# New operation orders on every engine, the three gelus of a step side by side, and TensorE's instruction alignment at place 92 of 256

## The chip, the cores and the metric

The kernel runs on 1 core of one Trainium2 chip. Its engines are TensorE (PE), VectorE (DVE), ScalarE (ACT), GpSimd (POOL) and SyncE (SP), each with an instruction stream of its own; they wait for each other through semaphores. The metric is the device time of one execution in microseconds; lower is better.

## The reference

The input is x of 8 sequences x 256 tokens x 128 channels. It is normalised to xn. The output is x + attention(xn) + local(xn). The first is one plain attention of width 128. The second is a stack of six layers, each of an attention over windows of 32 tokens and a gated feed-forward layer:

```python
for i in range(DEPTH):   # 6
    x = attn_layer(shift_tokens(x), Wqkv[i], q_scale[i], k_scale[i], Wo[i]) + x
    x = ffn_layer(shift_tokens(x), ln_g[i], ln_b[i], W1[i], b1[i], W2[i], b2[i]) + x
```

`attn_layer` projects to q, k and v (16 heads of 64), scales q and k to unit length, rotates them, takes a softmax over the window and the one before it, applies v, and projects out. `ffn_layer` normalises, projects to 2 x 341 channels (a and gate), multiplies a by gelu(gate) and projects down to 128. `shift_tokens` moves half of the channels by one token. All of it is fp32.

## The kernel before, in words

The plain attention is done first (about the first 50 us) and isn't touched. Then 48 **steps** follow, one for each layer and sequence: step n is layer n // 8 of sequence n % 8. A step's tokens are two tiles of 128. Every engine has a function `iteration(n)`, called for n = 0 to 52, in which the operations are written out by hand in a fixed order, each with the step that it belongs to: `hidden(n - 5, 1)` works on the step five back. So five or six steps are in flight, and an engine never takes an operation out of turn: one that waits holds up all behind it on its engine. `live(n)` leaves out steps that don't exist, at the beginning (the fill) and at the end (the drain).

TensorE's operations of a step, with the engine that takes each result:
- `take_in`: 2 transposes of the shifted tokens; `take_x` (ScalarE, L614) rounds them to x_hi, `rest` (VectorE, L883) writes the remainder x_lo, and signals s_xl.
- `project` 0 to 7 (q and k) and `project_v` 0 to 3: 3 matmuls of 128x512 each, in fp32r (hi x hi, hi x lo, lo x hi). q and k are squared on ScalarE (`square`), summed on VectorE (`squares`), rotated on VectorE (`rotate`, L894), added and scaled on GpSimd (`add`, `scale`); v is copied by ScalarE (`copy_v`) and moved by 32 tokens by SyncE's DMAs (`copy_v0`, `copy_v1`).
- `turn_qk` 0 to 7: 4 transposes each; ScalarE copies (`take_qk`, L646).
- `scores` 0, 1: 8 matmuls with the mask and 128 of 64x64 each; VectorE takes maxima (`maxima`, `less_max`), ScalarE the exponent (`exps`), VectorE sums and reciprocals, GpSimd divides.
- `turn_p` 0 to 3: 4 transposes; ScalarE copies (`take_p`).
- `values` 0 to 3: 32 matmuls of 64 columns; ScalarE copies (`take_o`, L691).
- `project_out` 0, 1: 16 matmuls; VectorE adds into x (`middle`). SyncE loads the shifted tokens (`load_xs`), VectorE takes statistics (`stats`, `moments`), GpSimd normalises.
- `turn_normal`: 2 transposes; `affine` on ScalarE.
- `hidden` 0 to 2: 4 matmuls; ScalarE's `gelu` (L706), VectorE's `gated` (L966), then `down` (12 matmuls) and `finish`.

A matmul of fp32 operands that is no transpose is issued as two, and each of those counted here has a weight load of its own; so a step has 544 matmuls and 544 weight loads, 36 of each in the projections, 272 in the two `scores`.

There are 8 PSUM banks. The constants `QK_BANK`, `T_BANK`, `H_BANK` and so on say which bank an operation writes, and `freed(...)` ahead of a TensorE operation waits until the last reader of that bank is done:

```python
def freed(*uses):
    for signal, n, *place in uses:
        if live(n):
            pe.wait_ge(signal, upto(place[0], n, place[1]) if place else done(n))
            return
```

ScalarE holds one table of functions at a time. Gelu is in one table; exponent, logarithm and the rest are in the other. `exp_and_log()` (L610) loads the second by hand; the load of the gelu table is put ahead of a gelu that finds another table (it has that gelu's line, L706). Squares and copies work with either.

TensorE's order before, from `take_in` (steps: 0 is n, -1 is n - 1 and so on): take_in 0; turn_qk 0 and 1 of -1; project 7 of -1; down -5; turn_qk 2 of -1; turn_p 1 of -2; project 0; turn_normal -4; values 0, 1 of -2; turn_qk 3 of -1; project_v 1 of -1; project 1, 2; project_v 0 and scores 0 of -1; hidden 0 of -4; project 3; turn_p 2, 3 and project_out 0 of -2; turn_qk 6 of -1; project 4; hidden 1 of -4; turn_qk 7, 4 of -1; and in the next iteration, up to its take_in: values 3, 2 of -3; turn_qk 5 of -2; project_v 3, 2 of -2; project 5 of -1; scores 1 of -2; hidden 2 of -5; project 6 of -1; turn_p 0 of -2; project_out 1 of -3.

## Time and profile before

| what | value |
|---|---|
| time, median of 3 runs | 1537.56 us (1534.16 to 1537.81) |
| the profiled execution: time, span | 1533.61 us, 1531.8 us |
| busy share of the span | PE 97%, PEld 83%, DVE 87%, ACT 90%, POOL 81% |
| matmuls, and as many weight loads | 26320 |

The span goes from the first to the last profiled instruction of one execution. PE is TensorE's matmuls, PEld its weight loads, which overlap them. Times in the timeline are us from the span's start; a row merges equal instructions (x4) and shows in brackets how long the engine was idle before it and what released it; "issue" means that nothing in the profile did.

### The profile page before, as it was taken

Reading aid. Unit: us, or ns where it says so; the run is one execution under the profiler, and the core shown is the slowest. Engines: PE = TensorE matmul, PEld = TensorE weight load, DVE = VectorE, ACT = ScalarE, POOL = GpSimd, SP = SyncE. Lnnn points to the kernel's source line nnn. Section 1 sums busy time; section 2 is a strip of 40 time slices with the busy share of each in tenths; the row PEclk is TensorE's granted clock in tenths of the full one; section 3 lists DMA queues with packets and bytes.
Section 4 is the critical chain, followed back from the end, with each engine's and each line's share of the span. In section 5 each row is a group of like instructions: output and inputs, shape, how many; then the busy total and the mean of one; then the engine's idle time right before and its main releaser. Section 6 shows DMA issues by size and latency. Waiting matters only on the chain.

```text
span 1531.8 us, 66396 instructions
## 1 busy us (share of the span) xinstructions
PE 1480.4 (97%) x26320; PEld 1278.3 (83%) x26320; DVE 1327.0 (87%) x2365; ACT 1381.5 (90%) x2647; POOL 1242.3 (81%) x1213
## 2 busy tenths in 40 slices
PE   6689999999999999999999999999999999999996
PEld 5568888888888888888888888888888888888885
DVE  6789998898989888988988898988889898889872
ACT  4578999999999999999999999999999999999996
POOL 5588888878888888888888888888888888887861
PEclk9999999999999999999999999999999999999998
DMA  6111221212121211222121213111121211111120
GB/s 181 36 44 44 54 54 51 53 35 57 48 61 52 67 39 42 61 58 62 45 59 34 54 48 80 51 49 49 35 53 42 63 35 48 37 47 44 40 53 19
DMA packets 96161, 79.89 MB, mean 52 GB/s; under 512 B 66282, under 2 KB 79598, under 8 KB 95854
## 3 DMA queue, kind: packets, MB, share of 16 engines
q1 hardware_dynamic: 94990, 75.34, 18.8%
q8 instruction: 217, 3.56, 1.0%
q14 instruction: 90, 0.74, 0.2%
q10 hardware_dynamic: 864, 0.26, 0.1%
HBM read 17.91 MB, written 1.05 MB: 12 GB/s over the span
## 4 chain that ended last, share of the span: by engine, by line
PE 91%; issue 4%; ACT 2%; DVE 2%; POOL 1%; DMA 0%; ACTq 0%; DVEq 0%; POOLq 0%
PE bank L1075 73%; PE bank L1190 11%; PE bank L1228 5%; PE bank L1160 1%; PE bank L1262 1%; DVE n L904 0%; DMA rot<-in_b_v 0%; ACT L611 0%; POOL rot L459 0%; ACT ot L691 0%; DVE es L935 0%; DVE parts L894 0%; DVE am L828 0%; ACTq L545 0%; POOL w_lo L446 0%
## 5 line engine op out<-in xcount | busy, mean ns | idle before, releaser
L459 POOL TENSOR_TENSOR rot<-parts 128x512 f32<-128x512 f32 x384 | 493.5, 1286 | 204.9 <-DVE parts L894 204.9
L894 DVE TENSOR_TENSOR parts<-bank,rtab 128x1024 f32<-128x1024 f32 x384 | 465.5, 1213 | 0.4 <-POOL rot L459 0.3
L470 POOL TENSOR_TENSOR rot<-rot,rnorm 128x512 f32<-128x512 f32 x384 | 391.0, 1046 | 0.4 <-DVE rnorm L920 0.4
L1075 PE MATMUL bank<-w_hi,x_hi 128*128 128x512 f32 x576 | 266.6, 463 | 7.4 <-DVE parts L894 4.9
L904 DVE TENSOR_REDUCE n<-sq 128x8 f32<-128x512 f32 x384 | 255.6, 667 | 18.6 <-ACT sq L622 18.6
L622 ACT ACTIVATE sq<-bank 128x512 f32<-128x512 f32 x384 | 231.3, 602 | 38.4 <-PE bank L1075 31.0
L684 ACT ACTIVATE pz<-bank 64x512 f32<-64x512 f32 x384 | 225.8, 588 | 3.8 <-PE bank L1228 0.4
L1075 PE MATMUL bank<-w_hi,x_lo 128*128 128x512 f32 x576 | 228.5, 397 | 0.0
L1075 PE MATMUL bank<-w_lo,x_hi 128*128 128x512 f32 x576 | 228.0, 396 | 0.0
L476 POOL TENSOR_TENSOR es<-es,r 128x512 f32<-128x512 f32 x192 | 200.5, 1045 | 28.3 <-DVE r L946 28.2
L1190 PE MATMUL bank<-ident,rot 128*128 128x128 f32 x1536 | 220.4, 276 | 2.3 <-POOL rot L470 1.8
L1075 PE MATMUL bank<-w_o,ot 128*128 128x128 f32 x1536 | 187.5, 275 | 0.0
L1190 PEld LDWEIGHTS bank<-ident,rot 128*128 128x128 f32 x1536 | 173.8, 141 | 15.8 <-issue 1.8
L1075 PEld LDWEIGHTS bank<-w_o,ot 128*128 128x128 f32 x1536 | 179.2, 192 | 0.5 <-issue 0.4
L935 DVE TENSOR_TENSOR es<-bank,m 128x512 f32<-128x512 f32 x192 | 127.5, 685 | 45.5 <-PE bank L1228 45.5
L646 ACT ACTIVATE kt<-bank 128x512 f32<-128x512 f32 x192 | 113.7, 592 | 53.2 <-PE bank L1190 52.4
L1075 PE MATMUL bank<-xg,w 128*128 128x256 f32 (+1 forms) x576 | 157.3, 396 | 4.3 <-DVE ht L970 2.2
L1075 PEld LDWEIGHTS bank<-kt,qt 64*32 64x32 f32 x12288 | 139.2, 105 | 10.7 <-issue 6.3
L1075 PE MATMUL bank<-kt,qt 64*32 64x64 f32 x12288 | 141.3, 225 | 5.5 <-issue 5.5
L929 DVE TENSOR_REDUCE m<-bank 128x8 f32<-128x512 f32 x192 | 126.5, 679 | 7.9 <-PE bank L1075 7.3
L1075 PEld LDWEIGHTS bank<-w_hi,x_lo 128*128 128x128 f32 x576 | 108.8, 189 | 26.6
L1075 PEld LDWEIGHTS bank<-w_hi,x_hi 128*128 128x128 f32 x576 | 109.1, 189 | 24.9 <-DVE parts L894 5.6
(86 smaller groups left out, 2799.9 us busy)
## 6 DMA issues: line engine op xcount, KB each, us to landing
vb<-v SPq DMA_DIRECT2D x96, 384.0 KB, 4.0
w_new<-in_Wqkv SPq DMA_DIRECT2D x36, 256.0 KB, 4.0
vb<-v SPq DMA_DIRECT2D x48, 128.0 KB, 2.6
w_o<-in_Wo SPq DMA_DIRECT2D x12, 256.0 KB
xin<-x_tok SPq DMA_DIRECT2D x48, 64.0 KB, 2.1
xs<-x_tok SPq DMA_DIRECT2D x48, 64.0 KB, 2.0
xin<-x_tok SPq DMA_DIRECT2D x48, 56.0 KB, 3.0
xs<-x_tok SPq DMA_DIRECT2D x48, 56.0 KB, 3.1
```

The costliest lines, as they stand in the source:

```text
L459: g.tensor_tensor(rot[:, i * CH:(i + 1) * CH].rearrange(halves, z=2, c=HD), parts[:, b:b + CH].rearrange(halves, z=2, c=HD), parts[:, b + ...
L470: g.tensor_tensor(c, c, over(r, CHH, DH), ALU.mult).then_inc(s_sc[i], 1)
L476: g.tensor_tensor(e, e, over(r8[:, (u % 2) * PAIRS:(u % 2 + 1) * PAIRS], PAIRS, DH), ALU.mult)\
L622: a.activation(sq[:, (i % 2) * CH:(i % 2 + 1) * CH], bank[QK_BANK[i]][:, :], ACT.Square)\
L646: a.activation(dst, bank[T_BANK[i]][:, :].rearrange("p (a t) -> p a t", a=4), ACT.Copy)\
L684: last = a.activation(pz4[r, u % 2, s, :], bank[P_BANK[u]][r, :], ACT.Copy)
L894: d.tensor_tensor(parts[:, b:b + 2 * CH].rearrange("p (w h c) -> p w h c", w=2, c=DH), heads(bank[QK_BANK[i]][:, :]).unsqueeze(1).to_broad ...
L904: d.tensor_reduce(n2[:, T * 2 * HEADS + m * CHH:T * 2 * HEADS + (m + 1) * CHH], heads(sq[:, b:b + CH]), op=ALU.add, axis=AX.X).then_inc(s_ ...
L929: d.tensor_reduce(eight(m8, u), heads(bank[S_BANK[u // 2][u % 2]][:, :]), op=ALU.max, axis=AX.X)\
L935: d.tensor_tensor(heads(es[:, (u % 2) * CH:(u % 2 + 1) * CH]), heads(bank[S_BANK[u // 2][u % 2]][:, :]), over(eight(m8, u), PAIRS, DH), AL ...
L1075: return t.matmul(o, l, r, start=start, stop=stop, skip_group_check=True)
L1190: last = t.transpose(bank[T_BANK[i]][:, k * P:(k + 1) * P], rot[:, i * CH + k * P:i * CH + (k + 1) * P], ident[:, :])
```

## The change

Every engine's order in `iteration` is written anew, with the banks and waits that belong to it. No arithmetic is added or taken away. ScalarE's three gelus now follow each other but for two copies, so that one load of the gelu table and one `exp_and_log` are left in a step. `align_block` is called from iteration 0 on, with 92 of 256 for 42 of 128.

TensorE's order after, from `take_in`: take_in 0; turn_p 1 of -2; project 6, 7 and turn_qk 0 of -1; project 0; down -5; values 0, 1 of -2; project 1; turn_qk 2, 1, 3 of -1; turn_normal -4; project_v 0 of -1; project 3; turn_p 2 of -2; project 2; project_v 1 and scores 0 of -1; project 4; turn_p 3 of -2; and in the next iteration, up to its take_in: project_out 0 of -3; turn_qk 4, 6, 5 of -2; values 2, 3 of -3; turn_qk 7 of -2; project 5 of -1; project_v 2 of -2; hidden 1 of -5; scores 1, turn_p 0 and project_v 3 of -2; hidden 2, 0 of -5; project_out 1 of -3.

VectorE's order after begins with the maxima of -2 and ends with squares 3 of n; `rest` stands behind gated 1, 2, 0 and squares 4. GpSimd's begins with scale 5, 7 of -2 and add 1 of -1 and ends with add 0 of n and scale 4, 6 of -1. The diff, cut to SyncE, ScalarE, and the parts of TensorE's order around the new alignment, hidden and down:

```diff
 DEEP = 5
-BLOCK, SLOT = 128, 42
+BLOCK, SLOT = 256, 92
 SPLIT_FROM = 2
 PARTS = ((0, 1), (1, 3), (3, SEQS))
-QK_BANK, T_BANK = (1, 3, 0, 5, 6, 5, 2, 3), (4, 5, 0, 6, 2, 3, 2, 7)
-V_BANK, P_BANK, O_BANK = (5, 4, 4, 1), (0, 4, 2, 7), (0, 7, 0, 4)
-S_BANK, W_BANK, H_BANK = ((6, 1), (7, 6)), (3, 3), (4, 1, 1)
-XIN_BANK, N_BANK, D_BANK = 1, 2, 1
-LAST_N2, LAST_SC = (3, 7), (3, 5)
+QK_BANK, T_BANK = (1, 3, 0, 7, 4, 2, 4, 0), (3, 4, 7, 2, 1, 6, 3, 6)
+V_BANK, P_BANK, O_BANK = (5, 1, 1, 1), (4, 5, 4, 3), (6, 5, 2, 0)
+S_BANK, W_BANK, H_BANK = ((6, 2), (6, 7)), (5, 2), (0, 3, 5)
+XIN_BANK, N_BANK, D_BANK = 3, 0, 2
+LAST_N2, LAST_SC = (2, 7), (3, 7)
...
@@ -382,15 +382,15 @@
                 if live(n):
                     load_x(n)
                 if live(n - 2):
-                    copy_v0(n - 2)
-                if live(n - 4):
-                    load_xs(n - 4)
-                if live(n - 2):
                     copy_v1(n - 2)
+                if live(n - 3):
+                    load_xs(n - 3)
+                if live(n - 1):
+                    copy_v0(n - 1)
                 if live(n - 5):
                     later_weights(n - 5)
-                if live(n - 2):
-                    later_qkv(n - 2)
+                if live(n - 1):
+                    later_qkv(n - 1)
...
             def take_x(n):
                 act.wait_ge(s_xt, done(n))
-                act.wait_ge(s_vp[2], done(n - 2))
+                act.wait_ge(s_vp[3], done(n - 2))
                 a.activation(buffer(x_hi, n, LEN), bank[XIN_BANK][:, 0:LEN], ACT.Copy).then_inc(s_xh, 1)
...
             exp_and_log()
 
             def iteration(n):
-                if live(n - 5):
-                    gelu(n - 5, 0)
-                if live(n - 1):
-                    square(n - 1, 3)
                 if live(n - 3):
-                    take_p(n - 3, 2)
                     take_p(n - 3, 3)
                 if live(n - 2):
+                    exps(n - 2, 0)
+                if live(n):
+                    next_hi(n)
+                if live(n - 2):
                     take_qk(n - 2, 6)
-                if live(n - 1):
+                    exps(n - 2, 1)
+                    take_qk(n - 2, 5)
+                    take_qk(n - 2, 4)
+                if live(n - 3):
+                    take_o(n - 3, 2)
+                if live(n - 1):
+                    guard(n - 1, 0)
                     square(n - 1, 4)
-                    guard(n - 1, 0)
+                if live(n - 2):
+                    take_qk(n - 2, 7)
+                if live(n - 1):
+                    square(n - 1, 5)
+                if live(n - 3):
+                    take_o(n - 3, 3)
+                if live(n - 1):
+                    logarithm(n - 1, 0)
+                if live(n - 2):
+                    copy_v(n - 2, 2)
+                if live(n - 1):
+                    first_root(n - 1, 0)
+                    half_square(n - 1, 0)
                 if live(n - 5):
                     gelu(n - 5, 1)
-                    exp_and_log()
-                if live(n - 1):
-                    logarithm(n - 1, 0)
-                if live(n - 2):
-                    exps(n - 2, 0)
-                if live(n - 3):
-                    take_o(n - 3, 3)
-                if live(n - 2):
-                    exps(n - 2, 1)
-                if live(n - 1):
-                    first_root(n - 1, 0)
-                    half_square(n - 1, 0)
-                if live(n - 2):
-                    take_qk(n - 2, 7)
-                    take_qk(n - 2, 5)
-                    take_qk(n - 2, 4)
+                if live(n - 2):
+                    take_p(n - 2, 0)
                     copy_v(n - 2, 3)
-                if live(n - 1):
-                    square(n - 1, 5)
-                if live(n - 2):
-                    copy_v(n - 2, 2)
-                if live(n - 3):
-                    take_o(n - 3, 2)
                 if live(n - 5):
                     gelu(n - 5, 2)
+                    gelu(n - 5, 0)
                     exp_and_log()
+                if live(n):
+                    take_x(n)
+                if live(n - 2):
+                    exps(n - 2, 2)
+                    take_p(n - 2, 1)
                 if live(n - 1):
                     square(n - 1, 6)
-                if live(n - 2):
-                    take_p(n - 2, 0)
-                if live(n):
-                    take_x(n)
-                if live(n - 1):
+                    square(n - 1, 7)
                     take_qk(n - 1, 0)
-                if live(n - 2):
-                    exps(n - 2, 2)
-                if live(n - 1):
-                    square(n - 1, 7)
+                if live(n):
+                    square(n, 0)
+                if live(n - 2):
+                    exps(n - 2, 3)
+                    take_o(n - 2, 0)
+                if live(n - 1):
+                    guard(n - 1, 1)
+                if live(n - 2):
+                    take_o(n - 2, 1)
+                if live(n - 1):
+                    logarithm(n - 1, 1)
                     take_qk(n - 1, 2)
-                if live(n - 2):
-                    take_p(n - 2, 1)
-                if live(n - 1):
                     take_qk(n - 1, 1)
-                    guard(n - 1, 1)
-                if live(n):
-                    square(n, 0)
-                if live(n - 1):
-                    logarithm(n - 1, 1)
                     first_root(n - 1, 1)
-                if live(n - 2):
-                    exps(n - 2, 3)
-                if live(n - 1):
                     half_square(n - 1, 1)
-                if live(n - 2):
-                    take_o(n - 2, 0)
-                if live(n - 1):
-                    take_qk(n - 1, 3)
-                if live(n):
-                    square(n, 1)
-                if live(n - 1):
-                    copy_v(n - 1, 1)
                 if live(n - 4):
                     affine(n - 4)
                 if live(n):
...
-            def align_block(n):
-
-                if live(n - DEEP):
-                    t.addr_align(BLOCK, offset=SLOT, max_nops=0)
+            def align_block():
+
+                t.addr_align(BLOCK, offset=SLOT, max_nops=0)
 
             def take_in(n):
                 pe.wait_ge(s_xin[n % 2], 64 * (n // 2) + 64)
...
-                if live(n - 2):
-                    freed((s_mid[0], n - 3), (s_rot[1], n - 1, 8, 1))
-                    turn_qk(n - 2, 5)
-                    freed((s_hm[1], n - 5), (s_sub[1], n - 2, 4, 1))
+                if live(n - 2):
+                    freed((s_qte[5], n - 2))
+                    turn_qk(n - 2, 7)
+                if live(n - 1):
+                    freed((s_ot[2], n - 3), (s_sub[1], n - 2, 4, 1))
+                    project(n - 1, 5)
+                if live(n - 2):
+                    freed((s_qte[4], n - 2))
+                    project_v(n - 2, 2)
+                if live(n - 5):
+                    freed((s_qte[6], n - 2),
+                          (s_pte[1], n - 3, 4, 3),
+                          (s_rot[1], n - 1, 8, 1),
+                          (s_qte[0], n - 2),
+                          (s_xl, n - 1),
+                          (s_hm[1], n - 6))
+                    hidden(n - 5, 1)
+                if live(n - 2):
+                    freed((s_qte[7], n - 2))
+                    freed((s_rot[1], n - 1, 8, 3), (s_qte[2], n - 2))
+                    scores(n - 2, 1)
+                    freed((s_rot[0], n - 1, 8, 4), (s_pte[0], n - 3, 4, 2))
+                    turn_p(n - 2, 0)
+                    freed((s_v[2], n - 2))
                     project_v(n - 2, 3)
-                    freed((s_ot[3], n - 3), (s_hm[0], n - 5), (s_v[1], n - 2))
-                    project_v(n - 2, 2)
-                if live(n - 1):
-                    freed((s_rot[1], n - 1, 8, 3))
-                    project(n - 1, 5)
-                if live(n - 2):
-                    freed((s_qte[7], n - 2))
-                    freed((s_rot[0], n - 1, 8, 4), (s_sub[0], n - 2, 4, 0))
-                    scores(n - 2, 1)
                 if live(n - 5):
-                    freed((s_v[3], n - 2), (s_hm[1], n - 5))
+                    freed((s_mid[0], n - 3),
+                          (s_v[0], n - 2),
+                          (s_ot[1], n - 3),
+                          (s_pte[1], n - 3, 4, 1),
+                          (s_hm[2], n - 6))
                     hidden(n - 5, 2)
-                if live(n - 1):
-                    freed((s_qte[4], n - 2))
+                    freed((s_ot[3], n - 3), (s_rot[0], n - 1, 8, 2), (s_xg, n - 5))
+                    hidden(n - 5, 0)
+                if live(n - 3):
+                    freed((s_rot[1], n - 1, 8, 5), (s_ot[2], n - 3))
+                    project_out(n - 3, 1)
+                if live(n):
+                    align_block()
+                    freed((s_hm[1], n - 5), (s_qte[6], n - 2), (s_pte[1], n - 3, 4, 3), (s_rot[1], n - 1, 8, 1))
+                    take_in(n)
+                if live(n - 2):
+                    freed((s_hm[2], n - 5), (s_mid[0], n - 3), (s_v[0], n - 2))
+                    turn_p(n - 2, 1)
+                if live(n - 1):
+                    freed((s_pte[0], n - 2, 4, 0), (s_rot[0], n - 1, 8, 4))
                     project(n - 1, 6)
-                if live(n - 2):
...
-                    freed((s_hm[2], n - 5),
-                          (s_v[3], n - 2),
-                          (s_hm[1], n - 5),
+                    freed((s_hm[0], n - 5), (s_ot[3], n - 3), (s_rot[0], n - 1, 8, 2))
+                    project(n - 1, 7)
+                    freed((s_xl, n), (s_hm[1], n - 5))
+                    turn_qk(n - 1, 0)
+                if live(n):
+                    freed((s_v[3], n - 2), (s_v[2], n - 2), (s_qte[4], n - 2), (s_v[1], n - 2), (s_rot[0], n - 1, 8, 0))
...
+                          (s_ot[2], n - 3),
                           (s_sub[1], n - 2, 4, 1),
-                          (s_rot[0], n - 1, 8, 0))
-                    take_in(n)
-                if live(n - 1):
-                    freed((s_v[2], n - 2))
-                    turn_qk(n - 1, 0)
-                    freed((s_rot[1], n - 1, 8, 5))
+                          (s_qte[3], n - 2),
+                          (s_xready, n - 6))
+                    down(n - 5)
+                if live(n - 2):
+                    freed((s_sub[0], n - 2, 4, 2))
+                    values(n - 2, 0)
+                    freed((s_pte[1], n - 2, 4, 1))
+                    values(n - 2, 1)
+                if live(n):
+                    freed((s_qte[0], n - 1), (s_xl, n))
+                    project(n, 1)
```

## Rows read from the trace of the kernel before

**Rows 1.** The page: busy time of the engines; the chain that ended last.
```profile
PE 1480.4 (97%) x26320; PEld 1278.3 (83%) x26320; DVE 1327.0 (87%) x2365; ACT 1381.5 (90%) x2647; POOL 1242.3 (81%) x1213
...
PE 91%; issue 4%; ACT 2%; DVE 2%; POOL 1%; DMA 0%; ACTq 0%; DVEq 0%; POOLq 0%
```

**Rows 2.** Timeline of TensorE at `take_in` of steps 6 and 47: start, length, instruction.
```profile
200.28 0.38 PE L1160 MATMUL bank<-ident,xin 128*128 128x128 f32 x2
...
1433.37 0.38 PE L1160 MATMUL bank<-ident,xin 128*128 128x128 f32 x2
```

**Rows 3.** Timeline of TensorE over one step.
```profile
801.23 0.38 PE L1160 MATMUL bank<-ident,xin 128*128 128x128 f32 x2
801.45 1.04 PE L1190 MATMUL bank<-ident,rot 128*128 128x128 f32 x8
...
802.79 0.40 PE L1075 MATMUL bank<-w_hi,x_lo 128*128 128x512 f32 x1
803.21 1.60 PE L1075 MATMUL bank<-w,ht 128*128 128x128 f32 x12
804.65 0.60 PE L1190 MATMUL bank<-ident,rot 128*128 128x128 f32 x4
805.09 0.60 PE L1228 MATMUL bank<-ident,es 128*128 128x128 f32 x4
805.44 0.48 PE L1075 MATMUL bank<-w_hi,x_hi 128*128 128x512 f32 x1
...
806.00 0.40 PE L1075 MATMUL bank<-w_hi,x_lo 128*128 128x512 f32 x1
806.23 0.38 PE L1262 MATMUL bank<-ident,xn 128*128 128x128 f32 x2
806.54 1.15 PE L1075 MATMUL bank<-pz,v 128*64 128x64 f32 x32
807.53 1.10 PE L1075 MATMUL bank<-pz,vb 128*64 128x64 f32 x32
...
811.62 0.40 PE L1075 MATMUL bank<-w_hi,x_lo 128*128 128x512 f32 x1
811.95 0.41 PE L1075 MATMUL bank<-mask,identh 64*32 64x512 bf16 x8
...
813.56 1.13 PE L1075 MATMUL bank<-xg,w 128*128 128x256 f32 x4
...
825.25 0.40 PE L1075 MATMUL bank<-w_hi,x_lo 128*128 128x512 f32 x1
825.78 0.41 PE L1075 MATMUL bank<-mask,identh 64*32 64x512 bf16 x8
...
831.25 0.38 PE L1160 MATMUL bank<-ident,xin 128*128 128x128 f32 x2
```

**Rows 4.** Timeline of the same step: ScalarE's x_hi, VectorE's x_lo, ScalarE's qt.
```profile
802.31 0.39 ACT L617 ACTIVATE x_hi<-bank 128x256 fp32r<-128x256 f32 x1
...
802.73 0.42 DVE L886 TENSOR_TENSOR x_lo<-bank,x_hi 128x256 fp32r<-128x256 f32 x1 [1.00 <-ACT x_hi L617]
...
824.50 1.08 ACT L646 ACTIVATE qt<-bank 128x512 f32<-128x512 f32 x2
```

**Rows 5.** Groups by line: table loads, count, busy time, mean ns.
```profile
L611 ACT ACT_TABLE_LOAD x97 | 124.5, 1283 | 1.7
```

**Rows 6.** Page's queues; waits (us in total, times, longest); timeline of TensorE.
```profile
q8 instruction: 217, 3.56, 1.0%
...
PE bank L1075 <- issue: 5.5, 5, 1.8
...
85.45 0.30 PE L1075 MATMUL bank<-kt,qt 64*32 64x64 f32 x3 [1.77 <-issue]
```

**Rows 7.** Timeline of the drain: a table load, and `down` of step 46.
```profile
1511.66 1.28 ACT L706 ACT_TABLE_LOAD   x1
...
1514.08 0.35 PE L1075 MATMUL bank<-w,ht 128*128 128x128 f32 x1 [2.07 <-DVE ht L970]
```

More of the change, by code:

```diff
@@ L1328, in iteration @@
                     turn_qk(n - 1, 1)
[L1329 to L1336 removed]
+                    freed((s_xready, n - 5), (s_mid[1], n - 3), (s_rot[1], n - 1, 8, 5))
```

224 lines of the change are left out of this document (96 added, 128 removed).

## The prediction, made before the changed kernel was run

> **What bounds the kernel now.** I read the page first. TensorE is busy for 97% of the span and holds 91% of the chain that ended last; VectorE has 87%, ScalarE 90%, GpSimd 81% [rows 1]. The reader is to see that four engines are loaded but one is full, so freeing another engine pays only where TensorE now waits for it. Then the timeline of TensorE, to find the period. `take_in` of sequence step 6 starts at 200.28 and that of step 47 at 1433.37 [rows 2]: 41 steps in 1233.1 us, 30.08 each. One ordinary step, 801.23 to 831.25, has 30.02 [rows 3]. Third, the starts inside that step, compared with what the same kind of neighbour costs elsewhere in it; a busy column hides short waits, because ends of matmuls are modelled and overlap the next start, but start-to-start times don't.
>
> Two places stand out. After the last matmul of a projection the next operation normally starts 0.23 us later (806.00 to 806.23). Ahead of `down` it is 0.42 (802.79 to 803.21) [rows 3], and x_lo, which `down` is made to wait for, is written by VectorE from 802.73 to 803.15, behind ScalarE's x_hi of 802.31 [rows 4]: a wait of 0.19. Ahead of the first `scores` it is 0.33 (811.62 to 811.95); ahead of the second 0.53 (825.25 to 825.78) [rows 3], and ScalarE's pair of qt copies, of which `scores` needs the last, runs from 824.50 to 825.58 [rows 4]: a wait of 0.20. So 0.39 us of the step are waits and 29.63 are TensorE's own work. That is the most a new steady order can win.
>
> **The work itself.** The diff changes no operation of TensorE, only its neighbours. I price them from the step. Transposes cost 0.11 each (801.23 to 801.45 for two, 804.65 to 805.09 for four), a projection 3 x 0.23, `down` 1.44 (803.21 to 804.65), a `values` about 1.0 (806.54 to 807.53), a `scores` 1.61 (811.95 to 813.56) [rows 3]. Changing from fp32r to fp32 work and back costs nothing I can see. Going into the small tiles of `values` or `scores` costs about 0.09: two transposes ahead of `values` take 0.31 (806.23 to 806.54) and not 0.22, and 0.33 stands for 0.23 ahead of `scores` [rows 3]. Before has four such entries a step (two pairs of `values`, two `scores`) and after has four too. Five neighbours are new and stand nowhere in the steady trace: down then values, values then project, hidden then scores, scores then turn, hidden then project_out. Each can be worth 0 to 0.1 either way, going by that entry. I take nothing for four and +0.07 in all, and keep -0.15 to +0.25 for the range.
>
> **ScalarE.** Now four table loads a step: the two of `exp_and_log` (97 at L611, 1.28 us each [rows 5]) and one ahead of the gelu that follows each of them. The three gelus side by side leave two, so 2.57 us a step go. ScalarE is not the bound, so that buys cover, not time: 2.57 of 30 us, 90% down to about 82%. The Trainium skill, "ScalarE: Activation LUTs", section "What ACT_TABLE_LOAD costs", puts a switch at about 1283 ns and a drain of about 1380 ns behind it. By that the saving would be about 5.3 us a step, an estimate from the page; the row has 1.28 for the load, and the time predicted is the same under either, since this engine is not the bound.
>
> **Do the new orders cover both waits?** I laid the new TensorE order from `take_in` = 0 with the prices above. `take_in` ends at 0.22, turn_p 1 and two projections end at 2.06, then turn_qk 0, which now carries the wait for x_lo. ScalarE starts about 0.2 after the transposes, x_hi to VectorE takes 0.42 (802.31 to 802.73), x_lo 0.42 and 0.06 more to TensorE [rows 4]: x_lo is there at 1.32. Cover 0.7, and `down` comes only at 3.2. For ScalarE to be free at 0.42: hidden 0 ends at -1.9, gelu 0 takes 0.5, the load 1.28, so it is free near 0.1. Cover 0.3, with 0.7 behind it. That is the tightest use of the freed time; with the two extra loads it would not fit. For the second `scores`, the copy of turn 7 ends near 21.9 and `scores` comes at 23.05: cover over 1 us. New tight place: project 5 reuses the bank of take_o 2. From the end of turn_qk 6 TensorE needs 0.44 + 0.09 + 2.0 + 0.41 = 2.95 us to reach it; ScalarE needs 0.2 + four operations of about 0.5 (two in 1.08 [rows 4]) + 0.6 for the take_o itself + 0.2 = 3.0. Cover about nothing, price 0.05, inside my +0.07. Behind that wait stand project_v 2, hidden 1 and scores 1, and VectorE's maxima wait for those. The GpSimd products that the turns read, and VectorE's rotations that free the banks, come out at least 0.7 us ahead of their use, most over 2; SyncE's copies of v are issued near 13.6 and read 20 us later, though they now stand behind load_xs in the queue.
>
> New step: 29.63 + 0.07 = 29.70. Saved: 41 x (30.08 - 29.70) = 15.6 us.
>
> **The fill.** 5.5 us in five pieces, the longest 1.8, are waits of TensorE for nothing but "issue". The first is seen at 85.45: `scores` stops with 3 of 128 matmuls left, for 1.77 [rows 6]; two more are like it at 99.65 (1.61) and 113.15 (1.44), together 4.8. The instruction queue moved 217 packets, 3.56 MB [rows 6], 16.4 KB each. TensorE has 26320 matmuls and as many weight loads [rows 1], with about 2200 waits 54,800 instructions: some 253 to a packet, so one packet is a block of 256. A `scores` is 272 instructions in 1.61 us, so it can run out of its block. I read these gaps as late instructions. The three are all in iterations ahead of the first alignment; after it stalls of this kind are rare. With alignment from iteration 0 at place 92, my count of the instructions from `take_in` (256 and about 19 waits to scores 0, then 511 more to scores 1) puts the block boundary near the 145th of 272 in both, far from either end. Since VectorE is nearly full there too, I take 3.5 of the 4.8, with 0 and 4.8 as ends.
>
> **The drain.** At the end nothing covers the gelus. Hidden 2 now shares a bank with hidden 1 and gelu 2 sits between two loads: one stands at 1511.66, and `down` at 1514.08 waited 2.07 [rows 7]. The same happens for the last step. With three banks and one load the last hidden sets the end: some 2 us less for step 46 and 1 for step 47. I take 3, with 0 and 6 as ends.
>
> **Sum.** 15.6 + 3.5 + 3.0 = 22.1. The profiled execution had 1533.6 (span 1531.8 and 1.8 around it), so 1511.5 in its terms; the median of the runs shown, 1537.56, is 0.26% above it, so 1515.5, rounded 1516.
>
> **Rivals.**
> A, slower: the jump costs a fetch. A step has 1133 TensorE instructions by my count. Before, it starts at place 42 or 170, so ends at 1175 or 1303 and jumps to 1194 or 1322, inside the same block of 256. After, it ends at 1225 and jumps to 1372, across 1280, every step. If the jumped-to block isn't there, TensorE stops as at 85.45, 1.4 to 1.8 us, 47 times: +66 to +83, about 1590. It decides above 0.47 us a jump (22.1 / 47). Against it: the next block is entered in order more than 5 us after the last, and a fetch gap is under 2. The Trainium skill, "Runtime: NRT & Kernel Launch", section "Instruction fetch mechanics", says that a taken branch to a target outside the current two-page window forces a fetch; the next block should be inside it, so by that rule too the jump would be free. No row of before shows such a crossing.
> B, a wait of the new order's own: one of the two thin covers (gelu 0, load, take_x, or take_o 2 ahead of project 5) is short by 0.5 us. 41 x 0.5 = 20.5 back: 1536, no change; slower if over 0.55. For it: ScalarE meets three gelus, a load, two copies in a row; against it: every one of them was costed by rows.
> C, the 0.39 are not waits but TensorE's own cost of those neighbours, and the orders win nothing: 1537.56 - 6.5 = 1531. Against it: the ends of x_lo and of the qt pair fit to 0.06 and 0.20 us.
>
> **How the numbers follow.** My case 0.62, A 0.08, B 0.16, C 0.14. A difference of 0.3% (4.6 us) is about what a measurement can tell here. Faster: 0.62, 0.09 of C, 0.02 of B: 0.73. Same: 0.05 of C, 0.09 of B: 0.14. Slower: A and 0.05 of B: 0.13. Low end: the neighbours at -0.15 (-6) and the ends of fill and drain (-4), less a little, since not all come together: 1507. High end: C and half of B, 1537. Own range of my case: 1507 to 1526.
>
> **What would show it.** `take_in` to `take_in` 29.6 to 29.9 us; `down` 0.23 behind its projection; two table loads a step, half as many at L611; no "issue" gap over 1 us in `scores`; no gap at `take_in`. Wrong if take_in waits for "issue" each step (A), if project 5 or turn_qk 0 waits for ScalarE or x_lo (B), or if the step stays at 30.0 without waits (C).

## The result, and the profile after

The changed kernel took 1501.83 us (median of 3 runs, 1499.92 to 1502.69); beside runs of the kernel before the ratio is 0.9777, 95% interval 0.9761 to 0.9792. 1516 was predicted, with 1507 to 1537 as the range: the direction was right, the size was not (35.7 us against 22). The profiled execution was the median one, 1501.83, its span 1500.0.

The page after, first the busy row and the chain that answer to [rows 1], then the instruction queue of [rows 6]:

```profile
PE 1464.2 (98%) x26320; PEld 1280.8 (85%) x26320; DVE 1310.1 (87%) x2365; ACT 1267.7 (85%) x2551; POOL 1248.7 (83%) x1213
...
q8 instruction: 241, 3.95, 1.1%
...
PE 93%; issue 2%; DVE 2%; POOL 1%; ACT 1%; DMA 0%; ACTq 0%; DVEq 0%; POOLq 0%
```

ScalarE lost 96 instructions and 114 us, TensorE did the same 26320 matmuls, and the queue moved 24 packets more: a step now takes five blocks of 256, and took four and a half. Table loads by line, against the 97 of [rows 5] (before had 96 more at the gelu's own line):

```profile
L616 ACT ACT_TABLE_LOAD x49 | 62.9, 1283 | 0.9
L711 ACT ACT_TABLE_LOAD x48 | 61.6, 1283 | 1.0
```

Then `take_in` of steps 6 and 47 in TensorE's timeline, the pair of [rows 2]:

```profile
199.56 0.38 PE L1149 MATMUL bank<-ident,xin 128*128 128x128 f32 x2
...
1411.54 0.38 PE L1149 MATMUL bank<-ident,xin 128*128 128x128 f32 x2
```

The span falls into three parts: until `take_in` of step 6, the 41 steps up to that of step 47, and what lies behind it.

| part | before | after | saved | predicted |
|---|---|---|---|---|
| fill | 200.3 | 199.6 | 0.7 | 3.5 |
| 41 steps | 1233.1 (30.08 each) | 1212.0 (29.56 each) | 21.1 | 15.6 |
| drain | 98.4 | 88.4 | 10.0 | 3.0 |
| span | 1531.8 | 1500.0 | 31.8 | 22.1 |

The remaining 3.9 us of the 35.7 are no part of these two profiles: before's profiled execution lay that much under the median shown, after's did not. Part of it may be the clock. Over the 45 executions of the kernel before that stand beside the experiments, the time goes with the mean granted clock of the whole execution, from 1530.8 us at 0.995 to 1541.3 at 0.988 (correlation -0.64); their mean is 1536.0 at 0.990, and the profiled one had 0.994.

The fill's 0.7 is within the scatter. `take_in` of step 0 comes at 50.0 and 50.4 us in two executions with the fill of before and at 51.1 to 53.2 in four with the changed kernel's (runs that alter the drain alone are among them); from there to `take_in` of step 6 it is 149.9 and 150.6 before and 147.5 to 148.9 after. So the fill itself is some 2 us shorter, and starts later.

TensorE's waits between 200 and 1411 us, which show nothing but the view's own head:

```profile
core 0 of [0], span 1500.0 us
engine line waited for: us in total, times, longest us
```

Start-to-start times agree. The beginning of one step after, for [rows 3], and ScalarE and VectorE at the next step's `take_in` (790.79), for [rows 4]:

```profile
761.22 0.38 PE L1149 MATMUL bank<-ident,xin 128*128 128x128 f32 x2
761.44 0.60 PE L1217 MATMUL bank<-ident,es 128*128 128x128 f32 x4
...
764.19 0.39 PE L1065 MATMUL bank<-w_hi,x_lo 128*128 128x512 f32 x1
764.42 1.50 PE L1065 MATMUL bank<-w,ht 128*128 128x128 f32 x12
765.85 1.15 PE L1065 MATMUL bank<-pz,v 128*64 128x64 f32 x32
```

```profile
789.70 1.28 ACT L616 ACT_TABLE_LOAD   x1
791.21 0.38 ACT L622 ACTIVATE x_hi<-bank 128x256 fp32r<-128x256 f32 x1 [0.23 <-PE bank L1149]
...
791.62 0.42 DVE L883 TENSOR_TENSOR x_lo<-bank,x_hi 128x256 fp32r<-128x256 f32 x1 [0.83 <-ACT x_hi L622]
```

`down` stands 0.23 behind its projection, where it was 0.42, and ScalarE is free 0.2 us before the bank of `take_in` is ready: x_lo is there 1.25 us after `take_in` (1.32 was predicted), 0.8 ahead of turn_qk 0, which now waits for it, and 2 ahead of `down`. Each of the 41 steps has 29.55 to 29.57 us; before, an ordinary one had 30.02, and a few had 30.4 to 30.6.

The drain, in TensorE's timeline, for [rows 7]; the bracket is idle time ahead and what ended it. First the kernel before, whole operations from `down` of step 46 on:

```profile
1514.08 2.59 PE L1075 MATMUL bank<-w,ht 128*128 128x128 f32 x12 [2.07 <-DVE ht L970]
1517.85 3.64 PE L1075 MATMUL bank<-xg,w 128*128 128x256 f32 x8 [0.75 <-ACT xg L699]
1522.57 1.09 PE L1075 MATMUL bank<-xg,w 128*85 128x256 f32 x4 [1.08 <-DVE ht L970]
1525.73 2.90 PE L1075 MATMUL bank<-w,ht 128*128 128x128 f32 x12 [2.06 <-DVE ht L970]
```

The same timeline of the changed kernel:

```profile
1484.71 2.83 PE L1065 MATMUL bank<-xg,w 128*128 128x256 f32 x12 [0.75 <-ACT xg L704]
1488.67 1.57 PE L1065 MATMUL bank<-w,ht 128*128 128x128 f32 x12 [1.13 <-DVE ht L967]
1491.28 2.83 PE L1065 MATMUL bank<-xg,w 128*128 128x256 f32 x12 [0.75 <-ACT xg L704]
1495.24 1.57 PE L1065 MATMUL bank<-w,ht 128*128 128x128 f32 x12 [1.13 <-DVE ht L967]
```

Two things changed above all. The waits of a step are 0.75 and 1.13, where they were 0.75, 1.08 and 2.07: for the two last steps 4.0 us less. And the same 12 matmuls of `down` take 1.57 and not 2.59 or 2.90, and the first 8 of the hiddens 3.64 where the step ahead (1507.88) has 1.97: 1.0, 1.3 and 1.7, another 4.0. Before also has one wait of 1.20 at 1473.71, ahead of `scores` and put down to ScalarE's kt, which after lacks. That makes 9.2 of the 10. Windows of before over these stretches have the granted clock (behind POOL's busy time) at 1.00, 0.86 and 0.64:

```profile
1480.00:1500.00 20.00, 19.09 (x360) 16.86 (x361) 9.47 (x23) 18.74 (x30) 6.57 (x8) 1.00 0.20 50
1500.00:1520.00 20.00, 15.04 (x129) 12.28 (x130) 5.59 (x18) 14.91 (x18) 4.98 (x8) 0.86 0.08 20
1520.00:1532.00 12.00, 5.48 (x20) 3.87 (x19) 2.30 (x5) 5.20 (x6) 0.00 (x0) 0.64 0.04 11
```

TensorE fell to the lower of its two levels (1.2 instead of 2.4 GHz) behind the waits of 2.07. My sum had counted waits alone. How much it falls differs between executions: in before_align_early (below), which is the same kernel from iteration 5 on, the hiddens of the last step take 1.96, the wait at `scores` is missing, and the drain is 95.8.

In the fill the clock was lower after than before. Waits after:

```profile
62.55 0.50 PE L1065 MATMUL bank<-w_hi,x_hi 128*128 128x512 f32 x1 [3.58 <-DVE parts L891]
66.76 1.09 PE L1179 MATMUL bank<-ident,rot 128*128 128x128 f32 x4 [2.40 <-POOL rot L470]
...
81.09 1.11 PE L1179 MATMUL bank<-ident,rot 128*128 128x128 f32 x4 [2.02 <-ACT qt L651]
```

Of the 4.8 us of "issue" waits in three pieces [rows 6], 0.8 in two are left behind 85 us, but 60 to 70 us had the clock at 0.70 (0.83 before) and 80 to 90 at 0.83 (1.00 before). The waits for VectorE and GpSimd between 60 and 70 us aren't new: before had 6.9 us of them in four pieces, after has 6.0 in two. New is the one of 2.02 for ScalarE's qt. And the clock between 60 and 70 us isn't a trait of the kernel: other executions with the same fill have 0.69, 0.83 and 0.98 there.

### The profile page after: what moved, and what is told of

Read it like the earlier page. It is cut to its first block, busy times and chain, and to the rows that moved or that the text cites. A ratio compares the mean times of both kernels' runs of the same rounds, so it can differ in the third digit from the quotient of the medians.

```text
span 1500.0 us, 66306 instructions
## 1 busy us (share of the span) xinstructions
PE 1464.2 (98%) x26320; PEld 1280.8 (85%) x26320; DVE 1310.1 (87%) x2365; ACT 1267.7 (85%) x2551; POOL 1248.7 (83%) x1213
## 4 chain that ended last, share of the span: by engine, by line
PE 93%; issue 2%; DVE 2%; POOL 1%; ACT 1%; DMA 0%; ACTq 0%; DVEq 0%; POOLq 0%
PE bank L1065 74%; PE bank L1179 11%; PE bank L1217 6%; PE bank L1251 1%; PE bank L1149 1%; DMA rot<-in_b_v 0%; POOL rot L459 0%; DVE parts L891 0%; DVE newton L910 0%; DVE s L937 0%; DVE n L901 0%; DVE am L825 0%; POOL w_lo L446 0%; ACTq L550 0%; ACT rot L576 0%
## 5 line engine op out<-in xcount | busy, mean ns | idle before, releaser
L891 DVE TENSOR_TENSOR parts<-bank,rtab 128x1024 f32<-128x1024 f32 x384 | 459.8, 1208 | 0.4 <-POOL rot L459 0.3
L1179 PE MATMUL bank<-ident,rot 128*128 128x128 f32 x1536 | 203.1, 275 | 5.0 <-POOL rot L470 2.4
L1065 PEld LDWEIGHTS bank<-w_o,ot 128*128 128x128 f32 x1536 | 182.8, 192 | 2.6
L1065 PE MATMUL bank<-xg,w 128*128 128x256 f32 (+1 forms) x576 | 139.8, 379 | 1.5 <-ACT xg L704 1.5
L696 ACT ACTIVATE ot<-bank 128x512 f32<-128x512 f32 x192 | 114.9, 599 | 25.9 <-PE bank L1065 20.9
L937 DVE TENSOR_REDUCE s<-es 128x8 f32<-128x512 f32 x192 | 129.7, 676 | 1.0 <-ACT es L681 1.0
```

Source lines behind the costliest of these rows:

```text
L891: d.tensor_tensor(parts[:, b:b + 2 * CH].rearrange("p (w h c) -> p w h c", w=2, c=DH), heads(bank[QK_BANK[i]][:, :]).unsqueeze(1).to_broad ...
L937: d.tensor_reduce(eight(s8, u), heads(es[:, (u % 2) * CH:(u % 2 + 1) * CH]), op=ALU.add, axis=AX.X)\
L1065: return t.matmul(o, l, r, start=start, stop=stop, skip_group_check=True)
L1179: last = t.transpose(bank[T_BANK[i]][:, k * P:(k + 1) * P], rot[:, i * CH + k * P:i * CH + (k + 1) * P], ident[:, :])
```

## The experiments

Each is timed beside the kernel before on the same chip, whose median was 1535.4 to 1536.9.

### Where the steady gain is from: ScalarE's relief or the order

**Relief in the old order.** In the kernel before, chunk 2 of the gate is an exponential and not a gelu, and the load behind it is left out. So there are two loads a step, TensorE's order is untouched, and the third chunk's hiddens are gated by another function.

```diff
-                a.activation(gt[0:w, j * LEN:(j + 1) * LEN], bank[H_BANK[j]][0:w, LEN:2 * LEN], ACT.Gelu,
+                a.activation(gt[0:w, j * LEN:(j + 1) * LEN], bank[H_BANK[j]][0:w, LEN:2 * LEN],
+                             ACT.Gelu if j < 2 else ACT.Exp,
...
-                    exp_and_log()
```

> The kernel before with ScalarE's third gelu of a step replaced by an exponential, and the load of the exponential table behind it left out: two table loads a step in the old order of TensorE's work. This changes part of the computation: the third chunk of hiddens is gated by an exponential. If ScalarE's two loads fewer are what won the steady part, the wait ahead of down in each step goes: step 29.65 to 29.75 instead of 30.08, and with a shorter drain 1515 to 1522. If the new order won it, the step stays at 30.00 to 30.08 and the time above 1530.

1517.75 us, ratio 0.9874 (0.9854 to 0.9894): 19 us come without any of the new order, of the 34 that the changed kernel has on the same chip. `take_in` 6 to 47 is 29.77 a step (30.08), an ordinary one 29.73 (30.02); the drain is 91.8 (98.4). TensorE's timeline, the second `scores` of one step and `down` of the next:

```profile
908.89 0.39 PE L1075 MATMUL bank<-w_hi,x_lo 128*128 128x512 f32 x1
909.43 0.41 PE L1075 MATMUL bank<-mask,identh 64*32 64x512 bf16 x8
...
916.45 0.40 PE L1075 MATMUL bank<-w_hi,x_lo 128*128 128x512 f32 x1
916.69 1.50 PE L1075 MATMUL bank<-w,ht 128*128 128x128 f32 x12
918.02 0.60 PE L1190 MATMUL bank<-ident,rot 128*128 128x128 f32 x4
```

ScalarE's timeline, behind `take_in` at 914.89:

```profile
915.31 0.39 ACT L617 ACTIVATE x_hi<-bank 128x256 fp32r<-128x256 f32 x1 [0.77 <-PE bank L1160]
```

The wait ahead of `down` is gone (0.24, was 0.42), and `down` itself takes 1.33 to the next start and not 1.44. Ahead of the second `scores` 0.54 stays. x_hi starts 0.42 behind `take_in`, where before it was 1.08 (801.23 to 802.31). So the loads kept ScalarE from `take_in`'s bank and made x_lo late. The rest, 29.73 to 29.56, is the new order's; that it is the wait for qt follows only from there being no wait left in the new one.

**The order without the relief.** In the changed kernel one more pair of loads a step, behind gelu 1:

```diff
+                    exp_and_log()
```

> The changed kernel with a load of the exponent table behind gelu 1, so that gelu 2 has to load its own again: four loads a step, as before, 2.57 us more on ScalarE between turn_p 0 and take_x. Theory (two loads fewer were needed for this order; cover there is 0.3 us ahead of take_x and 0.7 behind): x_lo comes about 1.5 us late for turn_qk 0, steady step near 31.1, 55 to 70 us slower than the changed kernel. Rival (ScalarE has 15% idle time and absorbs it): under 5 us.

1586.14, ratio 1.0330 (1.0311 to 1.0349), 31.20 a step: 84 us over the changed kernel, more than the 55 to 70 expected. The new wait in TensorE's timeline, and its total between 200 and 1400 us:

```profile
922.78 0.65 PE L1218 MATMUL bank<-ident,es 128*128 128x128 f32 x4 [1.25 <-DVE ht L968]
```

```profile
PE bank L1218 <- DVE ht L968: 49.3, 39, 1.3
```

Order and relief belong together: the new order needs the freed time, as forecast, though the wait came at turn_p 1, behind gated 2, and not at the places that I had called tight.

**Repairs within the old order.** `down` behind turn_qk 2 and turn_p 1; take_o 3 behind take_qk 4, so that qt comes earlier; both.

```diff
-                if live(n - 5):
-                    freed((s_xl, n), (s_hm[2], n - 5))
-                    down(n - 5)
...
+                if live(n - 5):
+                    freed((s_xl, n), (s_hm[2], n - 5))
+                    down(n - 5)
```
```diff
-                if live(n - 3):
-                    take_o(n - 3, 3)
...
+                if live(n - 3):
+                    take_o(n - 3, 3)
```

> The kernel before with one edit: on TensorE, down stands behind turn_qk 2 and turn_p 1, so that x_lo, which it is made to wait for, is there. Theory (the wait ahead of down is 0.19 us idle and 0.10 more in the first matmul of down, whose interval is 0.21 in the kernel before and 0.11 in the changed one): steady step 29.73, 41 x 0.29 = 12 us faster, if turn_qk 2 and turn_p 1 have no wait of their own. Rival 1 (only the idle time counts): 8 us. Rival 2 (0.42 is what that neighbour costs): nothing.

> The kernel before with one edit: on ScalarE, take_o 3 stands behind the last of the qt copies, not ahead of the first, so that the copy which the second scores waits for ends 0.48 us sooner. Theory: the wait of 0.22 us ahead of it goes, steady step 29.80, 9 us faster. Rival (something else is late there, such as a bank or GpSimd's work): under 3 us.

> The kernel before with both edits. Theory (the steady gain of the change is these two waits, and the orders could have been kept): steady step 29.5, 20 to 21 us faster than before, with four table loads a step still. Rival (ScalarE with four loads can't keep both covered: the second wait comes back elsewhere): 12 us or less.

1555.98, 1597.91 and 1618.59; ratios 1.0136 (1.0118 to 1.0153), 1.0411 (1.0390 to 1.0432), 1.0540 (1.0520 to 1.0561). None wins. Waits between 200 and 1400 us of the first and of the second:

```profile
PE bank L1075 <- DVE x_tok L977: 20.7, 40, 0.5
```

```profile
PE bank L1075 <- ACT ot L691: 54.4, 39, 1.6
```

All three were expected to win 9 to 21 us. In the first, the operation behind `down` now waits for x_tok:

```profile
819.70 0.50 PE L1075 MATMUL bank<-w_hi,x_hi 128*128 128x512 f32 x1 [0.52 <-DVE x_tok L977]
```

From `down` (817.68) to this start it is 2.02, where `down` without a wait takes 1.33: the wait of 0.52 costs 0.69, more than the 0.29 that was to be won, and an ordinary step goes from 30.02 to 30.50. The second makes ot late by 1.4 to 1.6. With four loads, each of these two moves brought a new and longer wait.

### The place in the block and the jump

The changed kernel with other places; the second kernel has 229.

```diff
-BLOCK, SLOT = 256, 92
+BLOCK, SLOT = 256, 150
```

> The changed kernel with place 150 of 256 in place of 92. By my count take_in then starts at 150, the step ends at 1283 and the jump goes to 1430, inside one block of 256, and the block boundary lies near the 87th of 272 instructions of each scores. Theory (a jump into the next block is free): time and steady step (29.56) the same within 1 us. Rival (the jump costs something in the changed kernel, hidden in the step): faster, by 47 times the cost.

> The changed kernel with place 229 of 256. By my count a block boundary then lies near the 8th instruction of each scores and the next one near the 264th. Theory (scores runs out of its block): an 'issue' gap of 1.4 to 1.8 us near the end of each scores, two a step, steady step 32.4 to 33.2, 1635 to 1675 us. Rival (the place in a block matters only now and then): under 1520 us.

At 92, by my count, the 1133 instructions of a step end at 1225 and the jump goes to 1372, into the next block. At 150 they end at 1283 and the jump to 1430 stays inside its block. A step has 29.56 in both, so the jump into the next block costs nothing. But the time is 1507.53, ratio 0.9813 (0.9797 to 0.9829): 5.7 more, in the drain (96.1), where two "issue" waits come, `down` of step 46 waits 2.34 instead of 1.13, and the clock is 0.85 between 1480 and 1500. TensorE's timeline there:

```profile
1454.02 0.31 PE L1065 MATMUL bank<-kt,qt 64*32 64x64 f32 x5 [1.87 <-issue]
...
1465.21 0.60 PE L1217 MATMUL bank<-ident,es 128*128 128x128 f32 x4 [1.42 <-issue]
```

At 229, by my count, each of the two `scores` has a boundary 3 instructions into its 272 and another at 259. It is 1585.6, ratio 1.0324 (1.0306 to 1.0341), with 31.47 a step; 1635 to 1675 was expected. Both stalls of a step in the timeline, and the total between 200 and 1400 us:

```profile
909.49 0.31 PE L1065 MATMUL bank<-kt,qt 64*32 64x64 f32 x7 [0.77 <-issue]
...
921.20 0.32 PE L1065 MATMUL bank<-kt,qt 64*32 64x64 f32 x8 [0.54 <-issue]
```

```profile
PE bank L1065 <- issue: 54.0, 76, 1.3
```

From start to start the first `scores` takes 2.64 (907.10 to 909.74) and the second 2.40 (919.05 to 921.45), where the changed kernel has 1.62 for either: 1.80 of the 1.91 that a step is longer. So two boundaries in one `scores` cost 0.95 us, and a single one 140 or 82 instructions in costs nothing. The stalls stand ahead of the last 7 or 8 matmuls, where the second boundary lies; what one boundary at either end would cost alone no run shows.

**Alignment early or late.** The changed kernel with alignment only from iteration 5 on, as before had it; and the kernel before aligned from iteration 0.

```diff
-                    align_block()
+                    if live(n - DEEP):
+                        align_block()
```
```diff
-                if live(n - DEEP):
+                if live(n):
```

> The changed kernel with the alignment from iteration 5 on, as before, and all else of the change. Theory (the three 'issue' gaps of the fill of before, 4.8 us, were late instructions, and early alignment removed them): scores in iterations 2 to 4 again falls on a bad place by chance; 0 to 5 us slower, with 'issue' gaps of 1.4 to 1.8 us inside scores before 120 us where it does. Rival (the fill was limited by VectorE and by the clock, so that the gaps were free): the gaps may come back, but the time is the same within 1 us. Steady step 29.56 in both.

> The kernel before with one edit: its alignment (42 of 128) from iteration 0 on. Theory: the three gaps of the fill (1.77, 1.61, 1.44 us) go, 3.5 us faster (0 to 4.8). Rival (the fill is limited elsewhere): under 1 us.

1502.04, ratio 0.9776 (0.9762 to 0.9791), and 1536.09, ratio 1.0000 (0.9987 to 1.0012): nothing either way. In the first, "issue" waits of 1.5 and 0.7 us in all came back behind 85 us. `take_in` 0 to 6 is 150.6 in its profile, 2 us over the changed kernel, but it began 2 us sooner, and the times are the same. In the second the stalls moved and weren't removed, so it doesn't tell what they cost; its waits from 40 to 200 us have three of them still:

```profile
PE bank L1075 <- issue: 4.6, 3, 1.8
```

### The drain and the clock

**Full clock in the old drain.** Matmuls that nobody reads, 4 ahead of hidden 2 and 8 ahead of `down`, in iterations 51 and 52 of the kernel before, into the free bank 5.

```diff
+            def busy(k, b):
+                for _ in range(k):
+                    mm(bank[b][:, :], w_hi[:, 0:P], w_hi[:, 0:CH])
...
+                    if n >= STEPS + 3:
+                        busy(4, 5)
...
+                    if n >= STEPS + 3:
+                        busy(8, 5)
```

> The kernel before, with matmuls that nobody reads in two gaps of TensorE in its last two iterations: 4 of 128x512 (0.93 us) ahead of hidden 2, 8 (1.87 us) ahead of down, into a free bank. Every output is computed as before. Theory (part of the drain's 10 us is the clock: in the kernel before the last down took 2.90 us and two hiddens 3.64, in the changed one 1.57 and 1.9): the granted clock stays at full speed and the kernel is 2 to 4 us faster than before. Rival (the clock falls for another reason, or the gaps are the cause alone): the same within 1 us or slower.

1529.42, ratio 0.9968 (0.9957 to 0.9979), 6.0 us less for 24 more matmuls (2 to 4 were expected). The last operations in its timeline, and its window:

```profile
1516.46 1.96 PE L1075 MATMUL bank<-xg,w 128*128 128x256 f32 x8 [0.75 <-ACT xg L699]
1519.51 1.09 PE L1075 MATMUL bank<-xg,w 128*85 128x256 f32 x4 [0.16 <-DVE ht L970]
1522.67 1.57 PE L1075 MATMUL bank<-w,ht 128*128 128x128 f32 x12 [0.21 <-DVE ht L970]
```

```profile
1500.00:1520.00 20.00, 17.64 (x150) 14.06 (x145) 6.56 (x20) 16.68 (x20) 4.99 (x8) 1.00 0.08 21
```

The fillers take the place of the waits and the hiddens take 1.96 instead of 3.64. From `down` of step 45 (1505.33 before, 1505.16 here) to the end it is 22.2 us and not 26.5: 4.2 us, the clock's part in these two profiles. The whole drain is 93.4, 5.0 less; the difference is ahead of the fillers, where this execution lacks the wait of 1.20.

**The old loads in the new drain**, an extra pair between gelu 2 and gelu 0, then also the shared bank (hidden 0 waits until gated 1 and 2 are done):

```diff
+                    if n >= STEPS + 2:
+                        exp_and_log()
```
```diff
+                    if n >= STEPS + 2:
+                        pe.wait_ge(s_hm[1], done(n - 5))
+                        pe.wait_ge(s_hm[2], done(n - 5))
```

> The changed kernel; in iterations 50 to 52 alone (steps 45 to 47) ScalarE loads the exponent table between gelu 2 and gelu 0, so that gelu 0 has to load its own again: four loads in each of these three steps. Theory (some 10 us of the change's gain lie behind take_in 47, and the loads between the gelus are a part of it): gelu 0 comes about 1.7 us later in steps 46 and 47, some more in 45 if nothing covers it; 3 to 6 us slower than the changed kernel. Rival (the drain was shortened by the order alone): under 1 us.

> As drain_loads, and in the same three iterations TensorE's hidden 0 waits for gated 1 and 2, as hidden 2 had to in the kernel before, where it shared a bank. Theory: hidden 0 starts after gated 2 and no longer beside gelu 1 and 2, down 6.2 us behind the first hidden in place of 4.0: 5 to 9 us slower than the changed kernel. Rival (the loads hide the bank's wait): as drain_loads, within 0.5 us.

1514.4 and 1511.1, ratios 0.9863 (0.9839 to 0.9886) and 0.9843 (0.9826 to 0.9861); drains 101.5 and 96.1, against 88.4. The loads alone were expected to cost 3 to 6 us. Their windows, loads alone first, with two operations of its TensorE timeline:

```profile
1480.00:1500.00 20.00, 13.10 (x55) 10.72 (x54) 4.74 (x14) 12.59 (x14) 2.49 (x4) 0.68 0.08 22
...
1483.47 2.66 PE L1067 MATMUL bank<-w,ht 128*128 128x128 f32 x12 [2.06 <-DVE x_tok L951]
1495.11 2.90 PE L1067 MATMUL bank<-w,ht 128*128 128x128 f32 x12 [3.34 <-DVE ht L969]
```

```profile
1480.00:1500.00 20.00, 12.64 (x72) 9.74 (x72) 5.41 (x15) 16.38 (x19) 2.49 (x4) 1.00 0.10 26
```

The kernel with more waits is the faster one in the median, though the intervals overlap. Its waits ahead of hidden and `down` are all under 1.9 us, and the clock holds until 1500; with the loads alone `down` waits 2.06, 3.34 and 2.61, and the clock is down from the first of them on. The loads cost 13 us here; the bank's share can't be read from this pair, since the clock moved with it. (The relief in the old order had the clock at 1.00 to the end: the 6.6 us that it saved in the drain are loads and the clock behind them. The other 3.4 of the 10 are the new order and its third bank.)

### The fill and the clock

The changed kernel with unread matmuls where TensorE waits in the fill: 14 ahead of project 6 and 9 ahead of turn_qk 0 in iteration 1; then 8 more ahead of turn_qk 7 in iteration 2. Each is followed by an alignment to where the program stood.

```diff
+                if n == 1:
+                    busy(14, 5)
+                    t.addr_align(BLOCK, offset=SLOT + 6, max_nops=0)
...
+                    if n == 1:
+                        busy(9, 5)
+                        t.addr_align(BLOCK, offset=SLOT + 20, max_nops=0)
...
+                    if n == 2:
+                        pe.wait_ge(s_v[0], 1)
+                        busy(8, 5)
+                        t.addr_align(BLOCK, offset=(SLOT + 405) % BLOCK, max_nops=0)
```

> The changed kernel, with matmuls that nobody reads in two gaps of the fill: 14 of 128x512 (3.3 us) ahead of project 6 and 9 (2.1 us) ahead of turn_qk 0 in iteration 1, each group followed by an alignment, so that the instructions behind stand as before. Every output is computed as before. Theory (the gaps are as long as before but lower the clock: 0.50 from 66 to 70 us): projections of 66 to 70 us take 0.7 and not 1.3 us, 1 to 3 us faster than the changed kernel. Rival (VectorE and GpSimd limit the fill, so that a faster TensorE only waits longer): the same within 0.7 us.

> The changed kernel once more, unaltered, beside the two versions below on the same chip, to price the fill. Both theories: 1501.8 us, steady step 29.56, take_in of iteration 6 at 199.6, 88.5 us behind the last take_in.

> The changed kernel with the unread matmuls of the fill (14 ahead of project 6 and 9 ahead of turn_qk 0 in iteration 1), which ended at 1500.9 once, with take_in of iteration 6 at 197.5 instead of 199.6. If the fill lost its gain to the half clock, this stays 1 to 2 us under the changed kernel in every round of the same chip (1500.3). If the fill's time is set by the waits themselves, the two agree within 0.3 us.

> The same with 8 more unread matmuls ahead of turn_qk 7 in iteration 2, in the stretch where TensorE waited 2.02 us for ScalarE's qt and the granted clock fell behind it. By the theory that the clock sets the fill: full clock to 90 us, about 1 us less again (take_in of iteration 6 at 196.5, about 1499.5). By the rival that ScalarE and VectorE set the end of the fill there: no change against busy_fill_again, a wait later on takes what is won.

The first version took 1500.91, ratio 0.9776 (0.9760 to 0.9792), which is the changed kernel's own, with `take_in` 6 at 197.5. On one chip, the unaltered kernel took 1503.05 (0.9773, 0.9758 to 0.9789), the first version 1501.83 (0.9764, 0.9748 to 0.9779), the second 1500.74 (0.9757, 0.9743 to 0.9770). Between 60 and 70 us, unaltered and second version:

```profile
60.00:70.00 10.00, 4.10 (x20) 2.86 (x19) 9.65 (x13) 3.87 (x11) 8.33 (x8) 0.98 0.00 0
```

```profile
60.00:70.00 10.00, 9.37 (x44) 7.02 (x43) 9.62 (x13) 4.51 (x11) 8.80 (x9) 1.00 0.01 3
```

The second version holds 1.00 from 60 us on; the unaltered kernel, at 0.98 here, has 0.83 from 70 to 90. The step down to 1500.7 is in the expected order and of the expected size, but the intervals overlap. `take_in` 0 to 6 is 146.8 and 147.8 in the two executions of the first version and 147.7 in the second's, against 147.5 to 148.9 without unread matmuls. That the second version is faster than the changed kernel is likely and not shown; both beat the kernel before.

## Why the prediction was right in sign and wrong in size

**The steady step, right mechanism, term mis-sized.** The failing sentence is "So 0.39 us of the step are waits and 29.63 are TensorE's own work. That is the most a new steady order can win." I had 30.02 - 0.19 - 0.20 + 0.07 = 29.70. Relief in the old order shows the first wait to be worth 0.29: 0.18 in front of `down` and 0.11 in its own intervals, which I had booked as work. The second, with the five new neighbours, was worth 0.17 where I had 0.20 - 0.07 = 0.13. So 29.56. Over 41 steps that is 5.5 us more than predicted.

**"That buys cover, not time", wrong for this pair of kernels.** I had taken the loads as help for the new order only. The chain to x_lo (`take_in`, ScalarE, VectorE, TensorE) ran through ScalarE's loads already, so relief alone wins 12.4 us in the steady part and 6.6 in the drain, with x_hi 0.42 behind `take_in` instead of 1.08. That ScalarE is at 90% and TensorE at 97% says nothing about this. The other half held: with four loads the new order is 84 us worse than with two.

**The drain, wrong: 3 predicted, 10 came.** I counted waits alone. Their part was nearly right: 4.0 us in the last two steps. What TensorE's clock does behind them I put at nothing: it is another 4.0 in the same rows, and 4.2 by the run with full clock in the old drain. A wait of 1.2 in the old `scores` came on top. How much of the 10 is the third bank alone stays open; with the new order it has at most the 3.4 that relief alone left.

**The fill, wrong: 3.5 predicted, 0.7 came, or some 2 from `take_in` 0 on.** The stalls for instructions went as forecast, 4.8 to 0.8, but time didn't follow them one for one. Between 40 and 200 us TensorE's other waits grew from 12.6 to 13.8, and in this pair of profiles the clock was lower from 60 to 90 us. In the changed kernel late alignment brings 2.2 us of stalls back at the same time. Why the rest is lost stays open; what the clock costs there is between nothing and some 2 us.

**The sum.** Steady part +5.5, drain +7.0 and fill -2.8 against the forecast, and the 3.9 between the profiles and the medians: 13.6 us more than the 22.1. I had scaled the result by 0.26% to before's median; the changed kernel's profiled execution is its median, so that addition was wrong too.

**The rivals.** A (a jump costs a fetch) fell: no wait in 41 steps, at 92 and at 150. The Trainium skill, "Runtime: NRT & Kernel Launch", section "Instruction fetch mechanics", forces a fetch only for targets outside the two-page window, and the jump into the next block agrees. Only the very first alignment shows: ahead of `take_in` 0 TensorE idles 1.07 to 1.09 us in the profiles with alignment from iteration 0 and 0.77 in those without, in both kernels, 0.3 us once. B (a wait of the new order's own) fell: none in the steady part. C (the 0.39 are TensorE's own) fell with 0.42 to 0.24 between the same neighbours. For the 0.20 ahead of the second `scores` no run has the same neighbours without the wait; there the step of 29.56, under the 29.63 that I called TensorE's own work, is the argument. What made the prediction miss was none of them; it was two terms counted in waits alone, and a fill whose stalls I took for time.

## What to carry to other kernels

Count a wait on a full TensorE by the interval in front and by those right behind it, and follow the chain that ends it through every engine: a table load on an engine that is not the bound can stand in it. In a drain ask what clock the waits leave behind them, and try unread matmuls in their place; in the fill of this kernel they won nothing clear. When instructions stream without loops, look where block boundaries fall in dense runs of small matmuls, and test the relief and the order apart before you credit either.

## What the runs showed of the hardware that was not expected

- Twelve unread matmuls an iteration, in the waits of the last two, made a kernel 6.0 us faster (granted clock 0.86 to 1.00 between 1500 and 1520 us).
- Block boundaries 3 instructions into `scores` and 13 before its end, by my count, cost 0.95 us together each time, in the steady part too; a single one near the middle costs nothing. The Trainium skill, "Runtime: NRT & Kernel Launch", section "Instruction fetch mechanics", has the crossing "mostly hidden"; with 272 instructions in 1.61 us, as `scores` has them, the run at place 229 says otherwise.
- After a table load the next operation of ScalarE starts 1.30 us behind its start (897.83 to 899.13 with relief in the old order), so no drain beyond the 1283 ns shows. The page "ScalarE: Activation LUTs" of the Trainium skill, section "What ACT_TABLE_LOAD costs", adds about 1380 ns; ScalarE's busy time fell by 114 us for 96 loads, 1.19 each, and not by 2.66.
